# Products of a tile of ones put between TensorE's prologue work in a one-core attention and mixture-of-experts kernel

## What is computed

```python
mod = (_silu(L0_c) @ L0_wmod).reshape(L0_c.shape[0], 6, 1, -1)
sa, ca, ga, sb, cb, gb = (mod[:, 0], mod[:, 1], mod[:, 2], mod[:, 3], mod[:, 4], mod[:, 5])
...
h = _layernorm(x, axis=-1) * (1 + ca) + sa
x = x + ga * _L0_attn_ref(h, ...)
h = _layernorm(x, axis=-1) * (1 + cb) + sb
x = x + gb * _L0_ffn_ref(h, ...)
# attention, per sequence of 512 tokens
scores = jnp.einsum('bqhd,bkhd->bhqk', xq, xk)
probs = jax.nn.softmax(scores.astype(jnp.float32), axis=-1)
out = jnp.einsum('bhqk,bkhd->bqhd', probs, xv).reshape(bsz, seqlen, dim)
return out @ wo.T
```

## Time and profile before

| | |
|---|---|
| median of 3 runs | 604.84 us (604.32 to 607.96) |
| the profiled execution's own time | 604.01 us, of which span 602.2 us |
| TensorE busy | 563.6 us, 94% of the span |
| VectorE busy | 370.8 us, 62% |
| ScalarE busy | 255.3 us, 42% |
| GpSimd busy | 217.8 us, 36% |
| mean granted TensorE clock | 0.974 |

### The profile page before, as it was taken

One profiled execution on the slowest core, in us unless ns is written; L12 is line 12 of the kernel. 1 busy time (PEld: TensorE's weight loads), 2 busy tenths in 40 slices (PEclk: granted clock), 3 DMA queues, 4 the chain that ended last, 5 costly groups with the idle time before them and its releaser, 6 DMA issues.

```text
span 602.2 us, 10736 instructions
## 1 busy us (share of the span) xinstructions
PE 563.6 (94%) x3118; PEld 313.8 (52%) x3119; DVE 370.8 (62%) x860; ACT 255.3 (42%) x519; POOL 217.8 (36%) x284
## 2 busy tenths in 40 slices
PE   4889999999999999999999999998999999999881
PEld 3443233333333333333343465668888898897570
DVE  6385677778589785898855569435444444443683
ACT  3113545564765647555568140022343443433000
POOL 6100000000110751108434653441675666667332
PEclk9966999999999999999999999999999999999996
DMA  7242126100501224012101169524555645540791
GB/s 227 42 132 97 34 54 188 37 11 10 115 4 34 93 70 115 7 31 90 53 1 41 66 267 330 147 82 130 158 157 151 182 144 165 166 124 9 269 371 58
DMA packets 42343, 67.18 MB, mean 112 GB/s; under 512 B 9291, under 2 KB 32212, under 8 KB 41948
## 3 DMA queue, kind: packets, MB, share of 16 engines
q1 hardware_dynamic: 30208, 45.62, 25.9%
q0 software_dynamic: 7680, 16.87, 8.2%
q10 hardware_dynamic: 4416, 4.20, 2.1%
HBM read 38.93 MB, written 27.51 MB: 110 GB/s over the span
## 4 chain that ended last, share of the span: by engine, by line
PE 81%; DVE 8%; issue 3%; DMA 3%; SPq 1%; ACT 1%; POOL 1%; ACTq 0%; POOLq 0%; DVEq 0%
PE ps L863 23%; PE ps L876 10%; PE ps L1089 9%; PE ps L1110 6%; PE ps L960 6%; PE ps L812 5%; PE ps L954 3%; PE ps L834 3%; PE ps L1075 3%; PE ps L821 3%; PE ps L889 3%; DVE max_q L1201 2%; PE ps L1100 2%; PE ps L798 2%; PE ps L919 1%
## 5 line engine op out<-in xcount | busy, mean ns | idle before, releaser
L1201 DVE TENSOR_REDUCE max_q<-ps 128x1 f32<-128x512 f32 x256 | 163.8, 686 | 74.5 <-PE ps L834 72.8
L691 ACT ACTIVATE probs<-ps 128x512 f32<-128x512 f32 x256 | 138.0, 596 | 99.5 <-PE ps L863 99.2
L834 PE MATMUL ps<-k_rows,q_rows 31*128 31x512 f32 x512 | 149.7, 678 | 1.8 <-DMA k_rows<-qk_raw 1.8
L863 PE MATMUL ps<-q_rows,k_rows 32*128 32x512 f32 x512 | 147.6, 646 | 0.9 <-DVE max_q L1201 0.9
L545 POOL DMA_INDIRECT results<-y_sb,dest x96 | 94.5, 984 | 64.8 <-issue 35.0
L863 PEld LDWEIGHTS ps<-q_rows,k_rows 32*128 32x128 f32 x512 | 42.9, 186 | 71.6 <-ACT probs L691 52.2
L1089 PE MATMUL ps<-up_sb,oT 128*128 x384 | 70.7, 328 | 1.5 <-DVE oT L1565 1.3
L876 PE MATMUL ps<-probs,v_ext 128*32 128x512 f32 x512 | 68.2, 605 | 1.1 <-ACT probs L691 1.1
L1089 PEld LDWEIGHTS ps<-up_sb,oT 128*128 128x128 f32 x384 | 61.4, 191 | 2.1 <-issue 1.9
L1110 PE MATMUL ps<-down_sb,e_hidT 96*128 x192 | 49.8, 383 | 3.8 <-ACT e_hidT L748 3.8
L498 POOL TENSOR_TENSOR rstd<-veps,mhalf 128x4 f32<-128x4 f32 x4 | 4.1, 1036 | 134.3 <-DVE veps L1283 132.4
(11 more groups left out here) (180 smaller groups left out, 695.7 us busy)
## 6 DMA issues: line engine op xcount, KB each, us to landing
xe<-dispatched SPq DMA_DIRECT2D x96, 129.0 KB, 2.1
up_sb<-results SPq DMA_DIRECT2D x16, 512.0 KB, 7.9
up_sb<-in_up SPq DMA_DIRECT2D x2, 3072.0 KB, 15.1
dispatched<-pad_rows SPq DMA_DIRECT2D x33, 129.0 KB, 4.5
down_sb<-in_down SPq DMA_DIRECT2D x1, 3072.0 KB, 31.3
x<-in_x ACTq DMA_DIRECT2D x4, 512.0 KB, 5.1
q_rows<-qk_raw SPq DMA_DIRECT2D x64, 32.0 KB, 1.9
k_rows<-qk_raw SPq DMA_DIRECT2D x64, 32.0 KB, 1.9
```

The costliest lines, as they stand in the source:

```text
L691: act.activation(probs[:, u % 8, :], ps[:, st_bank(t.b, g, u), :], ACT.Exp).then_inc(exp_done, 1)
L834: pe.matmul(ps[:, banks[u % len(banks)], :], q_rows[32 * i:32 * i + ONE, b % 2, g, qt * P:(qt + 1) * P], k_rows[32 * i:32 * i + ONE, b % 2 ...
L863: pe.matmul(ps[:, st_bank(b, g, n), :], k_rows[32 * i:32 * i + 32, b % 2, g, kt * P:(kt + 1) * P], q_rows[32 * i:32 * i + 32, b % 2, g, :] ...
L1201: dve.tensor_reduce(max_q[:, g % 2, qt, i:i + 1], ps[:, banks[(16 * g + n) % len(banks)], :], AXX, ALU.max).then_inc(max_done, 1)
```

## The change

GpSimd fills `ones` first, ahead of `ident`, and counts that on a semaphore of its own, `ones_s`, in place of its usual one; it waits for `ones_s` once more ahead of its first `consts`. TensorE waits for `ones_s` and then multiplies the 128x128 tile `ones` by itself into 128 columns of bank O, with no semaphore: 24 times ahead of the modulation's products, 4 times between the transposes and QK0, and once behind each of the 32 score products of the prologue. Nothing reads the results; the first product of L876 in turn 0 starts anew in that bank.

```diff
+        ones_s = sem("ones_s")
...
+            pool.memset(ones[:, :], 1.0).then_inc(ones_s, 1)
             st.did(pool.memset(ident[:, :], 0.0))
-            st.did(pool.memset(ones[:, :], 1.0))
             st.did(pool.memset(upper[:, :], 1.0))
...
             st.wait()
+            pool.wait_ge(ones_s, 1)
             pool.sem_inc(consts, 1)
...
         @block.tensor
         def _(pe):
+            def keep_awake(count):
+
+
+                for _ in range(count):
+                    pe.matmul(ps[:, O, 0:P], ones[:, :], ones[:, :], start=True, stop=True)
+
+            pe.wait_ge(ones_s, 1)
+            keep_awake(24)
             pe.wait_ge(mod_ld, 32)
             pe.wait_ge(c_ready, 1)
...
             for k in range(KD):
                 tokens_to_columns(lead, f"TP{k}", 0)
+            keep_awake(4)
             pe.wait_ge(qkv_ld, 48)
             for c in range(4):
                 project_qk(lead, c)
             for n in range(16):
                 score(0, 0, n, SC + ST[0:2])
+                keep_awake(1)
                 if n in (3, 7):
                     project_v(lead, n // 4)
             turn_max(lead, 3)
             for n in range(16):
                 score(0, 1, n, SC + ST[0:2])
+                keep_awake(1)
```

## The result

The changed kernel takes 671.13 us (median of 6 runs, 664.5 to 676.09) against 604.45 us for the kernel before (6 runs beside it). The ratio is 1.1055, 95% interval 1.1015 to 1.1095: 10.5% slower. The profiled execution took 671.57 us, its span is 669.8 us, 67.6 us more than before.

A forecast was written before the change was run, and what follows sets the result against it. TensorE, busy for 94% of the span, was taken to bound the kernel, and to set the scores' pace after the change. Terms -2.2 + 63 + 0 = +61 us gave span 663, median 666 us; 8-in-10 range 621 to 680.

The forecast's parts named there:

- The phases: Prologue scores: each score and its product of ones run one after the other, 1.44 us at 2.4 GHz, 2.68 at 1.2.
- The clock: Prologue scores: clock falls some 2 us in, V projections bring it back for a few us, group 1 wholly at 1.2 GHz.
- 69 - 6 = +63: Two groups of scores: 69 us more at 1.2 GHz, less 2 us before the fall and 4 us for the return.
- rows in use and not busy time: TensorE in the scores: array rows in use seem to keep the clock high; lone strips let it fall though TensorE is busy.
- The early products: First 28 products: raise the clock before QK0, so placing starts at 16.1 in place of 18.31, gaining 2.2 us.
- the term of -2.2 for the first score: Ahead of the scores: first score at 22.5 in place of 24.75 us; bounds +0.5 and -2.2.
- a case of up to 3 us: Rival, early part: clock not high at QK0, the 2.2 us lost, any case up to 3 us longer; no chance of its own.
- Turn 0: First steps after the scores: 3 us back if the clock is high on arrival; forecast low, so 0.

The follow-up runs named there:

- the repetition: The change itself, unaltered, run again beside the kernel before: 665.12 us against 604.31, ratio 1.103.
- the tuned version: Kernel before plus products of ones: 28 first, 9 ahead of the first score, two behind every fourth score, 5 per last-maxima wait; 601.38 us against 605.01.

## Why the prediction was right

**The phases, right.** The step that decided was that a product of all rows can't run beside a strip, so that each score pays for a phase of its own. It gave 1.44 us at 2.4 GHz and 2.68 at 1.2; measured are 1.47 and 2.73. The product in a strip, which costs nothing, and the 1.92 us with three products show the same from two other sides. The Trainium skill, "TensorE: Matmul & The Clock Gate", section "Part 3: Packing small matmuls — row/col tiling", has matmuls in strict order and weight loads pulled ahead only where row groups differ; the trace agrees: 1.07 us for four scores together, 4 x 1.47 with products of ones between.

**The clock, right in kind.** The prediction had it fall 2 us into the scores and return for 4 us of saving; it fell at 23.5 us, just ahead of the first score, and returned once, for 3.4 us. That early fall is a step the prediction didn't have: TensorE had been idle for 3.2 us. Without that wait (the products behind the scores alone) the clock fell 1.3 us into the scores, as forecast in kind. The term was 69 - 6 = +63, measured +67.5. The pace is 0.05 us slower in 30 intervals (+1.4), the V projections are 0.2 us shorter each than taken (-0.4), and what the clock gave back was 2.9 us and not 6: two scores at 2.4 GHz (1.26 each) and the end of the first V projection (3.08 in place of 3.41), nothing at the start. That makes 67.1, within 0.4 of the measured. In the repetition it stayed high for 13.6 us, so this part is different from run to run.

**What holds the clock.** The prediction took rows in use and not busy time. Three pairs bear it out: three products against one behind each score, two behind every fourth against none with the pauses filled, and the kernel before itself, whose clock fell under single scores. These show it for this kernel only; what the chip counts wasn't measured. Two rows limit it: products of all rows aren't needed (the clock came back at 47.8 us among products in strips alone), and three of them per score held the clock but didn't raise it. Idle time counts as well: TensorE waited about 3.2 us ahead of the first score in the change and with the first 28 products alone, and the clock fell at 23.5 and 22.9 us; in the kernel before, where it waited 1.8 us, it didn't. The rule of the Trainium skill, "TensorE: Matmul & The Clock Gate", section "Why this matters for your kernels", on idle gaps agrees with these places. It doesn't cover the lone strips, where the clock falls with no gap at all.

**The early products, half right.** They ended at about 9.1 us (8.5 to 9.5 forecast), QK0 began at 13.24 (13.4), and SP placed its first row at 16.10 (16.1). But the term of -2.2 for the first score was mis-sized: it came at 23.58, only 1.2 us earlier. SP's second issue took 1.63 us in place of 0.59. And the clock was taken as high at that score; in the longer wait for the rows it fell. So the early half is worth nothing by itself, which the text had only as a case of up to 3 us. That case was tied to the clock at QK0: in the repetition the clock did fall there, at 11.6 us, and the first score still came at 23.55.

**Turn 0.** Forecast 0, measured -1.0: the clock rose at 119.1, earlier in the first steps than before.

**The sum.** -1.2 + 67.5 - 1.0 = +65.3, and 2.3 us more in the expert stage give the 67.6 of the span; forecast was +61, and 666 us against a measured median of 671.13. The errors of the start (+1.0) and of the scores (+4.5) have the same sign; turn 0 (-1.0) takes part of them back, and the 2.3 us of the expert stage were in no term. The phases and a clock that is low in most of the scores were derived from rows; how long it returns inside the scores was a guess, and 10.5 us between two executions hang on it.

## What to carry to other kernels

Work put into a gap is free only if it fits the shape of what runs there: between matmuls that run side by side in strips of the array, one product of all rows turns four parallel products into four phases, here 0.60 us per score into 1.47 at 2.4 GHz and 2.73 at 1.2. Put such work behind a whole set of strips, or in the pauses, and count the places where it cuts, not the instructions. And check what a low clock costs before fighting it: here 3 to 4 us were to be had, and the fastest arrangement took 0.6%.

## What had not been expected of the hardware

- One product behind each of the 32 scores costs more than three, since three hold the clock: some 17 us between them.
- SP's second placement issue ends between 18.3 and 18.4 us in the profiled executions of the change and of the tuned version, whether it starts at 16.72 or at 17.36:

```profile
16.74 0.58 SPq L357
...
17.36 0.95 SPq L357
```

  These rows are of the tuned version; 16.72 for 1.63 us, above, is of the change. The other executions with the first 28 products are like one or the other, 16.82 for 1.54 us with three products and 17.38 for 0.94 in the repetition. The issue ahead of both is the transfer of `v_ext` into `k_rows` at 15.36. That it waits for that transfer is a guess; it wasn't tried. It takes back 1.0 of the 2.2 us that the early products win on SP.
- The early clock isn't sure either: in the tuned version it rose at 4.0 us, fell at 10.8 and rose at 14.2, and in the changed kernel it stayed high from 6.5 to 23.5. (The first rise, ahead of any record, is read from the number of products started: 7 in a us before it, 11 or 12 behind it.) Of the ten profiled executions with the first 28 products the clock fell between 10.8 and 12.1 us in the four in which TensorE had just waited 0.42 to 1.04 us for the tokens, and in none of the six in which it waited 0.17 us or less. That is a correlation; it wasn't tried. The windows of the tuned version:

```profile
9.00:12.00 3.00, 1.96 (x13) 1.90 (x13) 1.69 (x6) 1.68 (x5) 3.00 (x2) 0.80 1.07 361
12.00:15.00 3.00, 3.00 (x14) 2.58 (x13) 2.86 (x10) 1.49 (x2) 3.00 (x1) 0.63 0.10 30
```
